# Drain instructions in place of VectorE's waits for its own sums and maxima, in the edge passes of a four-layer graph network

## The reference

```python
# layer 0: two weighted sums over the edges
a_in  = segment_sum(feat_in[src] * iw[:, None], dst)
a_out = segment_sum(feat_out[dst] * ow[:, None], src)
# layers 1 and 3: rows of one of 8 relations, summed
out = segment_sum(t[etype, src], dst)     # layer 1
out = segment_sum(xt[etype, dst], src)    # layer 3
# layer 2: attention over the edges, with a loop at every node
alpha = leaky_relu(s_i[dst] + s_j[src], 0.2)
m = segment_max(alpha, dst)
a = exp(alpha - m[dst]); a = a / segment_sum(a, dst)[dst]
out = segment_sum(xj[src] * a[:, :, None], dst)
```

## Time and profile before

| | us |
|---|---|
| median of the three runs shown | 8612.98 |
| their range | 8594.42 to 8615.65 |
| span of the profiled execution | 8619.9 |
| `both_sums` (2515 to 3785) | 1270 |
| `aggregate`, layer 1 (4014 to 5213) | 1199 |
| `neighbour_max` (5362 to 6600) | 1238 |
| `aggregate`, layer 3 (7417 to 8584) | 1167 |

### The profile page before, as it was taken

The page is one execution under the profiler, slowest core; times in us unless marked ns, Lnnn a source line. Parts: engine busy times, 40 slices in busy tenths (PEclk is TensorE's granted clock), DMA queues, the critical chain, the costliest instruction groups (busy, mean ns, idle before and its releaser), DMA issues. The chain is left out here.

```text
span 8619.9 us, 69117 instructions
## 1 busy us (share of the span) xinstructions
PE 4852.2 (56%) x17004; PEld 2990.1 (35%) x17004; DVE 3573.0 (41%) x9196; ACT 1730.7 (20%) x7055; POOL 5243.4 (61%) x5610
## 2 busy tenths in 40 slices
PE   3202235555557777777455543777777876655554
PEld 1100014444435555543333332222223663333332
DVE  4201014333335555564222224444445776244445
ACT  0000001111123333322000002222223874000000
POOL 5577756666666666632666662666665882366665
PEclk6655557777778888888666666878888998866666
DMA  3001012222235555554333335656666884333333
GB/s 96 2 3 39 15 40 90 90 89 89 91 116 176 177 175 175 177 114 156 92 93 93 92 93 67 186 184 187 187 187 177 267 271 156 117 93 92 91 94 85
DMA packets 422550, 1037.69 MB, mean 120 GB/s; under 512 B 159993, under 2 KB 188189, under 8 KB 415516
## 3 DMA queue, kind: packets, MB, share of 16 engines
q0 software_dynamic: 223616, 552.46, 22.9%
q1 hardware_dynamic: 198556, 480.95, 17.4%
HBM read 716.74 MB, written 316.30 MB: 120 GB/s over the span
## 5 line engine op out<-in xcount | busy, mean ns | idle before, releaser
L944 POOL DMA_INDIRECT rel_rows<-relation_rows,rel_ring_row x1640 | 1558.3, 950 | 1177.7 <-ACT rel_ring_end L937 695.1
L956 PE MATMUL rel_sums<-rel_rows,rel_hot 128*128 128x256 f32 x3280 | 1197.1, 509 | 1178.3 <-issue 448.5
L956 PEld LDWEIGHTS rel_sums<-rel_rows,rel_hot 128*128 128x128 f32 x3280 | 785.7, 252 | 1590.1 <-issue 1076.9
L982 DVE TENSOR_TENSOR g_acc<-rel_sums,g_acc 128x256 f32 x1224 | 517.8, 423 | 1532.9 <-DMA records_by_dst<-g_big 548.5
L1913 POOL DMA_INDIRECT nmax_rows<-messages,nmax_ring_row x832 | 788.6, 948 | 566.3 <-ACT nmax_ring_row L1869 327.6
L761 POOL DMA_INDIRECT rows_by_src<-spread_rows,spread_ring_place x832 | 803.2, 965 | 483.8 <-issue 254.3
L838 POOL DMA_INDIRECT both_rows<-batch_normed,both_ring_row x832 | 791.0, 951 | 460.9 <-ACT both_ring_end L807 231.3
L605 POOL DMA_INDIRECT records_by_dst<-sort_ring_rec,sort_ring_place x784 | 810.4, 1034 | 390.6 <-issue 241.2
L739 PE MATMUL spread_p_r<-g_big,spread_hot_t 128*128 x1664 | 631.5, 545 | 542.0 <-ACT spread_hot_t L674 358.8
L1961 DVE TENSOR_TENSOR g_big<-nmax_short,g_big 128x512 f32 x832 | 575.7, 692 | 659.9 <-PE nmax_short L1934 288.6
L1934 PE MATMUL nmax_short<-nmax_rows,g_ident_b 128*128 128x512 bf16 x2496 | 800.3, 436 | 0.0
(11 more groups left out here) (443 smaller groups left out, 6114.8 us busy)
## 6 DMA issues: line engine op xcount, KB each, us to landing
kept_rows<-nmax_rows SPq DMA_DIRECT2D x208, 536.0 KB
g_big<-kept_rows SPq DMA_DIRECT2D x208, 536.0 KB
both_out_rows<-rows_by_src SPq DMA_DIRECT2D x202, 520.0 KB
att_local_row<-local_of_edge SPq DMA_DIRECT2D x52, 512.0 KB
rel_rows<-relation_rows,rel_ring_row POOLq DMA_INDIRECT x1640
relation_rows<-mix_table SPq DMA_DIRECT2D x25, 1024.0 KB
relation_rows<-fin_table SPq DMA_DIRECT2D x25, 1024.0 KB, 3.9
rows_by_src<-spread_rows,spread_ring_place POOLq DMA_INDIRECT x832
```

Of the source, the lines that this page charges most:

```text
L944: pool.indirect_dma_start(rows[:, j, 0:words], None, table, bass.IndirectOffsetOnAxis(ap=ring_row[:, j:j + 1], axis=0)).then_inc(landed[n ...
L956: last = nc.tensor.matmul(sums[:, unit % slots, 0:width], hot[:, j, :], rows[:, j, :], start=of == 0, stop=of == GRAIN[k] - 1)
L982: nc.vector.tensor_tensor(at, sums[:, unit % slots, 0:width], at, ALU.add).then_inc(added, 1)
```

## The change

Every wait of DVE for its own previous addition or maximum, inside the loops of the three functions, becomes `nc.vector.drain()`: an instruction on DVE's sequencer that ends when everything handed to the engine has been completed. The increments of `added`, `out_added` and `taken` stay, since PE waits on them. In `add_in` the condition on the first unit is dropped as well. `attend` keeps its wait. Lines behind 891 stand one line higher in the changed file.

```diff
             def add_out(n):
                 dve.wait_ge(out_summed, n + 1)
                 for unit in range(n * PER[1], (n + 1) * PER[1]):
                     if unit:
-                        dve.wait_ge(out_added, unit)
+                        nc.vector.drain()
                     at = target(1, g.acc2, unit)
                     nc.vector.tensor_tensor(at, out_sums[:, unit % 4, 0:width], at, ALU.add).then_inc(out_added, 1)
 
             def add_in(n):
                 dve.wait_ge(summed, n + 1)
                 for unit in range(n * PER[0], (n + 1) * PER[0]):
-                    if unit:
-                        dve.wait_ge(added, unit)
+                    nc.vector.drain()
                     at = target(0, g.acc[:], unit)
                     nc.vector.tensor_tensor(at, sums[:, unit % 4, 0:width], at, ALU.add).then_inc(added, 1)
...
                     if unit % 16 == 0:
                         tiles[:] = tiles_of(nc, mybir.EngineType.DVE, g, k, unit)
                     if unit:
-                        dve.wait_ge(added, unit)
+                        nc.vector.drain()
                     at = acc[:, bass.ds(tiles[unit % 16], 1), 0:width].rearrange("p t d -> p (t d)")
...
                 dve.wait_ge(scored, c + 1)
                 if c:
-                    dve.wait_ge(taken, c)
+                    nc.vector.drain()
                 at = high[:, bass.ds(tiles[unit % 16], 1), :, :].rearrange("p t h n -> p (t h) n")
```

## The result

The changed kernel took 8623.53 us (median of 20 runs), the kernel before 8604.05 (20 runs, 8594 to 8617): a ratio of 1.002, with a 95% interval of 1.0014 to 1.0026. The change costs 19.5 us by the medians, 12 to 22 by the interval. The sign of the forecast is right, and with this many runs the cost is clear of noise, but it is far from the +50 that was forecast.

The account below looks back on a forecast made before the run. The prediction took POOL's gathers, 5.0 us per group plus stops, to bound every pass. +55 us in `both_sums` and −5 in `neighbour_max` gave +50 on 8619.9, so 8670, less 6.9 to the median: 8663 us, range 8585 to 8745.

Parts of the forecast that it names:

- What bounds the kernel: All passes: POOL's gathers set a floor of 5.0 us per group; its stops add about 0.8 to 1.1.
- The price of a drain: At DVE's additions: the drain ends 10 to 50 ns after the operation; the register instruction now comes behind it.
- Held additions: Additions inside a run, waiting for a running predecessor: +0.06 us each, bounds 0 and +0.12.
- First ones: First addition of each run: loses its overlap and waits for whatever DVE runs, +0.30 us, bounds +0.10 and +0.36.
- A load behind the drain: Tile-number loads in `both_sums`: 1.13 us exposed, adding 0.03 us per group for "out" and 0.12 for "in".
- DVE's whole need: DVE's time per group in `both_sums`, loads included: from 4.29 to 5.27 us.
- The step that failed: `both_sums`: DVE's excess over POOL's floor charged in full, 0.26 × 208 = +55 us, bounds 0 and +204.
- rel1, rel3 and `neighbour_max` at 0, 0 and −5: Other passes: DVE's idle time hides dearer additions in rel1 and rel3; `neighbour_max` swaps semaphore instructions for drains, −5 us.
- DVE's late self-news: rel3: DVE seems to learn late of its own additions, 74.0 us in 100 waits; drains avoid this, gain taken as 0.
- No change: Rival, chance 0.31: dearer additions lie in POOL's stops, or drains end as early as semaphores came; 8608 to 8625 us.
- Faster: Rival, chance 0.13: drains cure late self-news in rel3, removing half of POOL's 149.6 us of stops there; 8538 us.
- Much slower: Rival, chance 0.06: `both_sums` follows DVE outright (+204 us) and rel3 loses part of its 97; 8866 us.

Follow-up runs that it names:

- the doses: Four or eight more comparisons per group for DVE in `both_sums`, into a scratch tile, against the kernel before: 8632 and 8661 us, each against 8601.
- The dose in the aggregates: One drain and four more comparisons per group in both aggregate passes, against the kernel before: 8626 against 8601 us, ratio 1.0018 to 1.0043.
- the filler: Kernel before plus a POOL memset of 512 columns behind each group's four gathers in `both_sums`: 8539.86 us against 8558, ratio 0.9972 to 0.9990.

## Why the prediction was right in its sign and wrong in its size

*What bounds the kernel.* POOL's 5.0 us per group plus its stops: right, and the table of stops adds up to the pace. Wrong was who makes the stops. The forecast took PE's 282.9 us of waits for DVE as proof that DVE does. But DVE was idle for 225 of them, and the row of its own waits has 179.0 us for late news ("remote"). On a chip without late news the same kernel's PE waits for DVE 0.3 us. Of POOL's 206 us of stops, 173 end late by news that was under way, and 33 are those that a slower DVE can add to.

*The price of a drain.* Held additions were put at +0.06 and took +0.04 (median gap 0.185 against 0.143 in rel3; 0.20 against 0.16 in the timeline of `both_sums`). First ones were put at +0.30 and took +0.28 (0.19 + 0.09). A load behind the drain was put at 1.13 on top of that and took 1.32 − 0.19 = 1.13. The sum per group without loads was put at 0.84 and is 0.74 (4.75 less 4.01). DVE's whole need, 5.27 forecast, is 5.24 where DVE sets the pace.

*The step that failed:* "I take the excess over POOL's floor as exposed: 0.26 × 208 = +55 us". It failed on the chips of the first kind, in size and in kind: measured in the profiles +20 (drains in `both_sums` alone against drains in the others alone) and +29 (the change), in the medians +16 and +19. The reason is in the prompt stops, which rose by 18 to 37 us while the late ones stayed at 154 to 173. Nor is it an excess over the floor that is charged there. The drains add some 0.9 us per group, about 190 us in the pass, and a tenth of that comes out; the doses come out at about a seventh, and one in the aggregates, where DVE with it needs at most 3.8 us per group, at a twentieth. On chips of the second kind, where POOL does run at 5.0, the step holds in kind: it gives 48 with the measured 5.24, and the change took 33.

*rel1, rel3 and `neighbour_max` at 0, 0 and −5:* right as a group (0 in the run with drains there alone). That DVE's late self-news would be cured and gain nothing was right too, though gaps of up to 2.38 us remain where none of several us was expected. The dose in the aggregates shows that their cover isn't complete.

*The rivals.* "No change" was nearest in size (within 0.3%, and the medians differ by 0.2%), and its argument, that the additions lie in POOL's stops, holds for most of their cost; the measured 8623.5 lies inside its 8608 to 8625. That is partly luck: the case counted from 8613, and 19.5 more than that is 8632, between this case and the forecast's 8640. "Faster" fell with the run on the other passes. "Much slower" did not occur on either kind of chip.

*Semaphore against drain.* The Trainium skill ("VectorE: DVE Perf Modes", section "The DRAIN you can't avoid") says that the next operation does not start until the pipe has emptied, and that one that is not held starts earlier. The trace agrees with the second half: an addition without a wait for the operation ahead started 0.09 us before that one's end. The section also has chained copies take as long with a semaphore after each as with one at the end. Here an addition that waited for its predecessor's semaphore started 0.14 to 0.16 behind its end, and one behind a drain starts 0.19 to 0.20 behind it, so a wait does move the start; copies were not run.

## What to carry to other kernels

A drain is dearer than a semaphore wait for the engine's own last result where that result has long been there: it waits for whatever runs on the engine, and takes the register work and loads behind it out of the overlap (0.28 us each here, up to 1.3 with a load, against 0.04 where the wait was real). Put it only where the predecessor really is still running. A wait of PE for DVE does not show that DVE is slow: look at whether DVE worked or waited in that time. And before an excess over the busiest engine's pace is charged in full, look at what ends that engine's stops: here over four fifths of the stops' time before, and 70% of it with the drains, ended by news that came late, and a dose of harmless work on the suspected engine shows in one run what its time is worth.

## What the runs showed of the hardware

- On some chips PE's semaphore updates were recorded, and answered by ACT, up to 13.1 us after the rows of PE's matmuls had ended, in 87 of 203 groups of `both_sums` by over 1 us; on others never by more than 0.04. The sum fell from 441 to 67 us in the kernel where DVE sets the pace and POOL stops 134 times in place of 98, but a pause of 0.7 us in each group (the filler) left it at 482; what it hangs on was not found. Where it occurs, the kernel before takes 12 to 13% longer (8558 to 8604 against 7627); that the lateness is all of that difference was not tested.
- DVE hears of its own additions late in rel3 on such chips: the one that ended at 7791.03 has its update recorded at 7796.74. Gaps between two additions of a group reached 5.92 us; with drains the longest was 2.38, and there the sequencer's register instructions took 0.3 to 1.4 us. Why they did was not found.
- A drain ended 0.05 us after the operation it waited for (3122.612 against 3122.564), and the next addition started 0.19 to 0.20 after that operation, with a register instruction of 65 to 75 ns in between.
- Giving the busiest engine 0.4 us more work per group of one pass made the kernel 18 us faster on one kind of chip.
